# The experts' element work reordered, the router's tail moved behind the first expert's values, and the weighted down biases taken in one fp32r pass

## What is computed

```
x = x + attention(layernorm(x))
x = x + context_attention(layernorm(x), ctx, mask)
h = layernorm(x)                                  # the part that the change touches
logits = h @ router_weight.T + router_bias        # 512 x 16
top_val, top_idx = top_k(logits, 4)
scores = zeros.at[top_idx].set(softmax(top_val))  # 512 x 16, 4 of a row are not zero
gate, up = split(h @ gate_up[e] + gate_up_bias[e])
gate, up = min(gate, 7), clip(up, -7, 7)
out[e] = ((up + 1) * gate * sigmoid(1.702 * gate)) @ down[e] + down_bias[e]
x = x + sum over e of scores[:, e] * out[e]
```

## Time and profile before

| | us |
|---|---|
| median of 3 runs | 227.85 (227.73 to 227.97) |
| the profiled execution | 227.91 |
| its span, first to last instruction | 225.8 |
| around the span | 2.1 |
| PE busy | 215.7 (96%) |
| DVE busy | 176.1 (78%) |
| ACT busy | 125.6 (56%) |
| POOL busy | 84.3 (37%) |

### The profile page before, as it was taken

One profiled execution on the slowest core, in us unless ns is written; L12 is line 12 of the kernel. 1 busy time (PEld: TensorE's weight loads), 2 busy tenths in 40 slices (PEclk: granted clock), 3 DMA queues, 4 the chain that ended last, 5 costly groups with the idle time before them and its releaser, 6 DMA issues. The chain is left out here.

```text
span 225.8 us, 4387 instructions
## 1 busy us (share of the span) xinstructions
PE 215.7 (96%) x1394; PEld 175.9 (78%) x1394; DVE 176.1 (78%) x433; ACT 125.6 (56%) x248; POOL 84.3 (37%) x70
## 2 busy tenths in 40 slices
PE   7999999998997998899999999999999999999995
PEld 2688767776685987698797888888888887887894
DVE  3579887777768546888979879879879889889865
ACT  2239789778533219266466476385384484484540
POOL 6359989001011010443444435435426426425000
PEclk9999999999999999999999999999999999999999
DMA  6894420000000000040340340430421422310002
GB/s 181 328 378 140 141 86 0 0 4 0 3 0 0 3 0 1 0 142 20 122 129 12 139 126 17 139 101 38 139 77 62 139 64 75 139 46 0 0 0 93
DMA packets 7997, 17.41 MB, mean 77 GB/s; under 512 B 928, under 2 KB 3120, under 8 KB 7856
## 3 DMA queue, kind: packets, MB, share of 16 engines
q1 hardware_dynamic: 7552, 16.94, 22.9%
q10 hardware_dynamic: 432, 0.31, 0.4%
HBM read 16.72 MB, written 0.52 MB: 76 GB/s over the span
## 5 line engine op out<-in xcount | busy, mean ns | idle before, releaser
L307 POOL TENSOR_TENSOR WLg<-raw_g,WHg 128x1024 fp32r<-128x1024 f32 x16 | 38.3, 2394 | 49.8 <-ACT WHg L407 49.6
L837 DVE SCALAR_TENSOR_TENSOR pt<-pt 128x512 f32<-128x512 f32 x30 | 49.4, 1648 | 4.2 <-DVE pt L833 1.8
L536 ACT ACTIVATE HH<-pt 128x512 fp32r<-128x512 f32 x30 | 19.0, 632 | 53.1 <-DVE pt L837 53.0
L1155 PE MATMUL PS<-XH,WHg 128*128 128x512 f32 x120 | 47.0, 392 | 0.7 <-ACT pt L527 0.7
L1155 PE MATMUL PS<-XL,WHg 128*128 128x512 f32 x120 | 46.9, 391 | 0.0
L1155 PE MATMUL PS<-XH,WLg 128*128 128x512 f32 x120 | 46.7, 389 | 0.0
L1171 PE MATMUL PS<-WHd,HH 128*128 128x256 f32 x120 | 35.3, 294 | 1.5 <-DVE HL L842 1.1
L1171 PE MATMUL PS<-WLd,HH 128*128 128x256 f32 x120 | 33.9, 283 | 0.0
L1171 PE MATMUL PS<-WHd,HL 128*128 128x256 f32 x120 | 33.9, 283 | 0.0
L842 DVE TENSOR_TENSOR HL<-pt,HH 128x512 fp32r<-128x512 f32 x30 | 22.2, 739 | 11.0 <-ACT HH L536 11.0
L314 POOL TENSOR_TENSOR WLd<-raw_w,WHd 128x512 fp32r<-128x512 f32 x15 | 19.7, 1315 | 28.4 <-ACT WHd L413 28.3
(11 more groups left out here) (157 smaller groups left out, 349.2 us busy)
## 6 DMA issues: line engine op xcount, KB each, us to landing
raw_g<-we_d SPq DMA_DIRECT2D x16, 512.0 KB, 4.0
raw_w<-we_d SPq DMA_DIRECT2D x16, 256.0 KB, 2.7
ctxT<-ctxT_d SPq DMA_DIRECT2D x1, 1024.0 KB, 10.0
ctx_sb<-ctx_d SPq DMA_DIRECT2D x1, 1024.0 KB, 12.1
wqkv<-wqkv_d SPq DMA_DIRECT2D x3, 256.0 KB, 5.0
out_d<-x SPq DMA_DIRECT2D x4, 128.0 KB, 1.8
rows<-rows_d SPq DMA_DIRECT2D x1, 264.0 KB, 6.3
x<-x_d ACTq DMA_DIRECT2D x2, 128.0 KB, 3.2
```

The lines of the kernel that those rows point to most:

```text
L307: g.tensor_tensor(WLg[slot][:, :, :, :].rearrange("p k g f -> p (k g f)"), raw_g[slot][:, :], WHg[slot][:, :, :, :].rearrange("p k g f -> ...
L536: a.activation(HH[slot][:, m, :], hid[:, m, :], ACT.Copy).then_inc(hh_done, 1)
L837: v_.scalar_tensor_tensor(out=hid[:, m, :], in0=glu[:, m, :], scalar=GLU_MAX, in1=upc[:, m, :], op0=ALU.min, op1=ALU.mult).then_inc(hid_do ...
L1155: i = t.matmul(PS[:, 2 * m + part, :], w[slot][:, k, part, m * P:(m + 1) * P], xx[:, k, :], start=(n == 0), stop=(n == 3 * KD - 1))
```

## The change

1. **DVE's order in an expert** becomes product(0), product(1), low(0), low(1), and then all four of the weighted sum. **ACT's** becomes high(0), high(1), and only then the rounding of the gate_up weights of expert e + 2.
2. **The router's tail** (L810 to L817 of before) moves into expert 0's element work, behind low(1): it is `rest_of_router`.
3. **The exponential** is taken through a function that shares the GELU's table: with t = tanh(x / 8), ((1 + t) / (1 - t)) squared twice is exp(x). This adds six small DVE instructions. The table is loaded by name after the last exponential of the context attention.
4. **The scores and biases** get 80 rows in place of 16: scores high at rows 0 to 15, low at 32 to 47, high again at 64 to 79; biases high, high, low at the same rows. Both are fp32r, so that one product over 80 rows gives the three terms. DVE writes the score parts (three instructions), SP brings the biases three times, POOL clears the gaps and splits them (memsets at its start, three instructions 80x256 between its first and second `rstds`).
5. **PE** turns the scores behind down(0) (bank 6 in place of 5) and multiplies by the biases behind the first half of gate_up(2); DVE starts the accumulator in expert 1, behind low(1).

```diff
@@ SP @@
-            sp.dma_start(dbias[:, :], dbias_d).then_inc(dbias_in, 16)
+            sp.wait_ge(dbias_zero, 1)
+            for block in range(3):
+                sp.dma_start(dbias[block * 32:block * 32 + E, :], dbias_d).then_inc(dbias_in, 16)
@@ POOL @@
+            g.memset(dbias[:, :], 0.0).then_inc(dbias_zero, 1)
+            link(g.memset(low_rows[:, :], -1.0))
+            link(g.memset(low_rows[0:64, :], 0.0))
+            g.memset(score3[:, :, :], 0.0).then_inc(score3_zero, 1)
...
-            for n in range(1, 5):
-                rstds(n)
+            rstds(1)
+            pool.wait_ge(dbias_in, 48)
+            g.tensor_copy(dbias_high[:, :], dbias[:, :]).then_inc(dbias_split, 1)
+            pool.wait_ge(dbias_split, 1)
+            g.tensor_scalar(dbias_high[:, :], dbias_high[:, :].bitcast(F32), low_rows[:, 0:1], None, ALU.mult).then_inc(dbias_split, 1)
+            pool.wait_ge(dbias_split, 2)
+            g.tensor_tensor(dbias3[:, :], dbias[:, :], dbias_high[:, :].bitcast(F32), ALU.add).then_inc(dbias_split, 1)
+            rstds(2)
...
@@ ACT @@
             context_take(3)
+            a.preload_act_table_set("gelu_apprx_sigmoid_and_others")
...
-            a.activation(elog[:, :, :], dlog[:, :, :], ACT.Exp).then_inc(elog_done, 1)
+            a.activation(elog[:, :, :], dlog[:, :, :], ACT.Tanh, scale=0.125).then_inc(elog_done, 1)
...
                 high(0)
+                high(1)
                 if not isinstance(e, int) or e + 2 < E:
                     high_gate_up(e + 2, slot, pair + 1)
-                high(1)
@@ DVE @@
-            link(v_.tensor_tensor(within[:, :, :], rank[:, :, :], need[:, :].unsqueeze(2).to_broadcast([P, NC, E]), ALU.is_le))
...
+            def rest_of_router():
+
+                dve.wait_ge(elog_done, 1)
+                v_.tensor_scalar(root[:, :, :], elog[:, :, :], -1.0, 1.0, ALU.mult, ALU.add)
+                link(v_.tensor_tensor(within[:, :, :], rank[:, :, :], need[:, :].unsqueeze(2).to_broadcast([P, NC, E]), ALU.is_le))
+                v_.reciprocal(esel[:, :, :], root[:, :, :])
+                link(v_.tensor_tensor(sel_eq[:, :, :], eq[:, :, :], within[:, :, :], ALU.mult))
+                v_.scalar_tensor_tensor(out=root[:, :, :], in0=elog[:, :, :], scalar=1.0, in1=esel[:, :, :], op0=ALU.add, op1=ALU.mult)
+                link(v_.tensor_tensor(sel[:, :, :], sel_eq[:, :, :], gt[:, :, :], ALU.add))
+                link(v_.tensor_tensor(esel[:, :, :], root[:, :, :], root[:, :, :], ALU.mult))
+                link(v_.tensor_tensor(elog[:, :, :], esel[:, :, :], esel[:, :, :], ALU.mult))
...
+                link(v_.tensor_copy(high.bitcast(F32R), score[:, :, :]))
+                v_.tensor_tensor(low_, score[:, :, :], high, ALU.subtract)
+                v_.tensor_copy(again, high).then_inc(score_done, 1)
...
                 product(0)
+                product(1)
+                low(0)
+                low(1)
                 if isinstance(e, int) and e == 0:
+                    rest_of_router()
                     dve.wait_ge(scoreT_ps, 1)
-                    v_.tensor_copy(scoreT[:, :], PS[0:E, 5, :]).then_inc(scoreT_done, 1)
-                low(0)
-                product(1)
...
+                    v_.tensor_copy(scoreT[:, :], PS[0:ROWS3, 6, :]).then_inc(scoreT_done, 1)
+                if isinstance(e, int) and e == 1:
                     for c in range(NC):
                         dve.wait_ge(dbias_ps, c // 2 * 2 + 2)
...
-                else:
-                    weighted_sum(e - 1, 1 - slot, (0, 1))
-                    low(1)
-                    weighted_sum(e - 1, 1 - slot, (2, 3))
+                if not isinstance(e, int) or e >= 1:
+                    weighted_sum(e - 1, 1 - slot, range(NC))
@@ PE @@
-                    i = t.transpose(PS[0:E, 5, c * P:(c + 1) * P], score[:, c, :], ident[:, :])
+                    i = t.transpose(PS[0:ROWS3, 6, c * P:(c + 1) * P], score3[:, c, :], ident[:, :])
...
-                    if m == 0 and isinstance(e, int) and e == 1:
-                        turn_scores()
+                    if m == 0 and isinstance(e, int) and e == 2:
+                        weighted_biases()
...
+                down(e, slot)
                 if isinstance(e, int) and e == 0:
-                    weighted_biases()
-                down(e, slot)
+                    turn_scores()
```

More of the change, by code:

```diff
@@ L37 @@
 DW = D * KD
+ROWS3 = 2 * 32 + E
 def decoder_layer(nc, x_d, ctx_d, ctxT_d, wqkv_d, wo_d, params_d, rows_d, mask_d, dbias_d, we_d, out_d):
@@ L69, in decoder_layer @@
         mask8 = sb("mask8", [P, B * M], U8)
-        dbias = sb("dbias", [E, D])
+        dbias = sb("dbias", [ROWS3, D])
+        dbias_high = sb("dbias_high", [ROWS3, D], F32R)
+        dbias3 = sb("dbias3", [ROWS3, D], F32R)
+        low_rows = sb("low_rows", [ROWS3, 1])
         raw_g = [sb(f"raw_g{i}", [P, GU]) for i in range(2)]
@@ L133, in decoder_layer @@
         elog = sb("elog", [P, NC, E])
+        root = sb("root", [P, NC, E])
         esel = sb("esel", [P, NC, E])
@@ L137, in decoder_layer @@
         score = sb("score", [P, NC, E])
-        scoreT = sb("scoreT", [E, T])
+        score3 = sb("score3", [P, NC, ROWS3])
+        scoreT = sb("scoreT", [ROWS3, T], F32R)
         XH = sb("XH", [P, KD, T], F32R)
@@ L199, in decoder_layer @@
         out_done = sem("out_done")
+        dbias_zero, dbias_split, score3_zero, score_parts = (sem(n) for n in ("dbias_zero", "dbias_split", "score3_zero", "score_parts"))
         XS_BANK, XT_BANK, XV_BANK = (7, 2, 4, 5), (3, 4, 6, 3), (1, 2, 4, 5)
@@ L372, in _ @@
             split_keys(1)
-            for n in range(1, 5):
-                rstds(n)
+            rstds(1)
[6 more added lines that the diff above has]
+            rstds(2)
+            rstds(3)
+            rstds(4)
             def expert(e, slot, pair):
@@ L809, in _ @@
             link(i)
-            link(v_.tensor_tensor(within[:, :, :], rank[:, :, :], need[:, :].unsqueeze(2).to_broadcast([P, NC, E]), ALU.is_le))
-            link(v_.tensor_tensor(sel_eq[:, :, :], eq[:, :, :], within[:, :, :], ALU.mult))
-            link(v_.tensor_tensor(sel[:, :, :], sel_eq[:, :, :], gt[:, :, :], ALU.add))
-            dve.wait_ge(elog_done, 1)
-            link(v_.tensor_tensor(esel[:, :, :], elog[:, :, :], sel[:, :, :], ALU.mult))
-            link(v_.tensor_reduce(etot[:, :], esel[:, :, :], AX.X, ALU.add))
@@ L816, in _ @@
-            link(v_.reciprocal(erec[:, :], etot[:, :]))
-            v_.tensor_tensor(score[:, :, :], esel[:, :, :], erec[:, :].unsqueeze(2).to_broadcast([P, NC, E]), ALU.mult
-                             ).then_inc(score_done, 1)
+            def rest_of_router():
[8 more added lines that the diff above has]
+                link(v_.tensor_tensor(elog[:, :, :], esel[:, :, :], esel[:, :, :], ALU.mult))
+                link(v_.tensor_tensor(esel[:, :, :], elog[:, :, :], sel[:, :, :], ALU.mult))
+                link(v_.tensor_reduce(etot[:, :], esel[:, :, :], AX.X, ALU.add))
+                link(v_.reciprocal(erec[:, :], etot[:, :]))
+                link(v_.tensor_tensor(score[:, :, :], esel[:, :, :], erec[:, :].unsqueeze(2).to_broadcast([P, NC, E]), ALU.mult))
+                dve.wait_ge(score3_zero, 1)
+                high, low_, again = (score3[:, :, n * 32:n * 32 + E] for n in range(3))
+                link(v_.tensor_copy(high.bitcast(F32R), score[:, :, :]))
+                v_.tensor_tensor(low_, score[:, :, :], high, ALU.subtract)
+                v_.tensor_copy(again, high).then_inc(score_done, 1)
@@ L1141, in turn_scores, with weighted_biases @@
                 for c in range(NC):
-                    i = t.transpose(PS[0:E, 5, c * P:(c + 1) * P], score[:, c, :], ident[:, :])
+                    i = t.transpose(PS[0:ROWS3, 6, c * P:(c + 1) * P], score3[:, c, :], ident[:, :])
                 i.then_inc(scoreT_ps, 1)
+            def weighted_biases():
+                pe.wait_ge(scoreT_done, 1)
+                pe.wait_ge(dbias_split, 3)
+                for c in range(NC):
+                    t.matmul(PS[:, 6 + c // 2, (c % 2) * D:(c % 2 + 1) * D], scoreT[:, c * P:(c + 1) * P], dbias3[:, :], start=True, stop=True
+                             ).then_inc(dbias_ps, 1)
             def gate_up(e, slot):
@@ L1175, in down @@
                         i.then_inc(y_done, 1)
-            def weighted_biases():
-                pe.wait_ge(scoreT_done, 1)
-                pe.wait_ge(dbias_in, 16)
-                for c in range(NC):
-                    t.matmul(PS[:, 6 + c // 2, (c % 2) * D:(c % 2 + 1) * D], scoreT[:, c * P:(c + 1) * P], dbias[:, :], start=True, stop=True
-                             ).then_inc(dbias_ps, 1)
             def both(e, slot, pair):
```

1 line of the change is left out of this document (removed).

## The result

The kernel after takes 222.43 us (222.38 to 222.54, four runs) against 227.91 (227.73 to 228.24) for the kernel before in runs on the same chip: a ratio of 0.9759, with a 95% interval of 0.9742 to 0.9775. The forecast was 223.2, its range 220.7 to 226.0. The profiled execution took 222.38 us with a span of 220.7, against 227.91 and 225.8.

The account below looks back on a forecast made before the run. PE was taken to bound the kernel, paused each expert by a DVE, ACT and POOL ring; 1.59 - 0.48 - 0.25 + 3.82 = 4.68 us less gave 223.2 us, range 220.7 to 226.0 (80%).

Parts of the forecast that it names:

- accumulator's wait: In expert 1, down(1) waits for the accumulator's start at the end of DVE's list: 0.25 us lost, between 0 and 1.0.
- fourteen pairs: gate_up and down of experts from gate_up(2) on: 8.35 us a pair in place of 8.62, 3.82 us gained in all.
- Part 1: Expert loop: new order of element work on DVE and ACT removes PE's pause before down, 3.82 us gained.
- part 3: Expert 0: low(1) ends at 89.90, so down(0) runs from 91.7 to 94.6 without a wait; before, it started at 95.86.
- Part 2: Table load moves into ACT's idle stretch: expert 0's work comes 1.30 us earlier, PE's 0.69 wait goes, gate_up(1) at 86.2.
- Part 4: Behind down(0), PE waits 2.1 us for the scores (96.7); gate_up(2) starts at 97.25 against 98.84, 1.59 us gained.
- the hold: Router's tail: POOL's subtractions delay DVE rows reading two SBUF tiles; without this, the sum is 2.15 us lower.
- rival B: Router's tail: small DVE instructions aren't held by POOL, so PE has no pause before the scores; 221.0 us, 17%.
- C: Loop's seam: the 0.27 us pause is the price of wait values from registers and stays; 226.85 us, 15%.
- D: PE's pause at 94.6: the clock falls to its lower level; one pair at that level gives 231.6 us, 5%.
- E: Loop's first experts: part of the pause stays, where DVE is still late after the tail; 224 to 226 us, 8%.

Follow-up runs that it names:

- experiment 1: Kernel before with DVE's and ACT's new orders: 223.05 us; with DVE's alone: 224.17 us (profiled 223.34); with ACT's alone: 227.63 us.
- experiment 3: Kernel after with expert 1's down-weight subtraction behind the scores: 221.54 us; also with only 8 of 1024 columns subtracted for expert 2's gate_up: 220.76 us.
- experiment 8: Kernel before with 2080 unused bytes a partition ahead of the accumulator in SBUF: ratio 1.0009; its profiled execution took 228.43 us at mean clock 0.991.

## Why the prediction was right, step by step

| | forecast | measured |
|---|---|---|
| gate_up(1) starts | 86.2 | 86.03 |
| down(0) | 91.7 to 94.6 | 91.49 to 94.4 |
| scores there | 96.7 | 96.02 |
| turning | 0.5 | 0.39 |
| gate_up(2) earlier by | 1.59 | 2.37 |
| bias product | 0.48 lost | 0.47 |
| accumulator's wait | 0.25 lost | 0.12 |
| fourteen pairs, biases and wait apart | 3.82 gained | 3.89 |
| last addition to span's end | no change | 0.56 lost |
| around the span | no change | 0.43 gained |
| profiled time less by | 4.68 | 5.53 |

The two rows on the span's end weren't in the sum at all. That they nearly cancel is luck.

**Part 1** has the right size, and its mechanism half. That product(1) must not stand behind low(0) is shown (experiment 1); that ACT's late rounding, by taking POOL out of DVE's way, is part of the gain is refuted: with or without it the pair is 8.34. In the stretch ahead of gate_up(2) the order gives a further 0.66 (98.18 in place of 98.84 with the orders alone), which my sum had under part 3. So DVE's order alone brings the last block 4.6 us forward (219.56 to 214.97), and all the rest of the change, which is most of its lines, 1.1 (to 213.89).

**Part 2** held, where its experiment could be read. **Part 3** held to 0.2.

**Part 4** is the term that was mis-sized, by 0.78 us of the 0.85 that the sum missed. The held rows came as forecast, two of them, one for each POOL instruction. But POOL began 0.15 earlier than I had it and was done at 93.70, not 94.1; the rows that followed took 2.3, not 2.6 (they are ten, where I had counted eleven); and the turning 0.39, not 0.5. A slip without weight: 227.91 less 4.68 is 223.23, not 223.25. The price of the hold, with the tail in this place, is what the kernels of experiment 3 give back by their medians: 0.9 us without the second held row, 1.7 without either; by their ratios 1.0 and 2.0. gate_up(2) came 1.7 us earlier in the second, counted from gate_up(1). I had 2.15.

The Trainium skill's "SBUF — State Buffer", section "Who interferes with whom", gives no size from which its exclusion holds. The trace agrees with it down to 128x64 (2.05 us in place of 0.2), and rival B, that small rows escape, fell. With one SBUF input the reciprocal ran beside POOL undisturbed (0.55 with and without it), while the clip of 128x512, which has one too, was held (1.32 in place of 0.43). The same section has both: it exempts a single input, save in a mode with two ports, and counts tensor_scalar among the operations that can enter it.

**The rivals.** C (register waits make the seam's pause) fell: the loop still takes its wait values from registers and runs at 8.34, and in experiment 8 so do three of its pairs in the old order. D (the clock) fell for this kernel: 1.0 in all its four runs, with a pause of 1.55 us. But its argument against D, that the waits of before left no mark on the clock, held for one trace only: in experiment 8 the clock fell in a wait of 0.84 us, and the kernel without the early table load had one run at 0.854 and 238.94 us. E fell, since even the first pair behind gate_up(3) took 8.34.

## What to carry to other kernels

A pause of 0.2 us at each turn of a loop shows neither in PE's waits nor in its busy share. The page has only a hint of it, the idle time of PE's weight loads in front of down: 7.3 us before, 0.8 after. So subtract starts of blocks, and compare a turn that is unrolled with one in the loop. Where DVE and GpSimd meet on SBUF, look first at what stands behind the held instruction, because an order that does the multiplies of both halves before the first dependent step makes a hold of the same length harmless. Such a loop also hides what PE loses elsewhere, so a gain in front of it may only show once the loop is mended. Before moving work out of the way of a hold, follow what sets the other engine off: in two of the kernels above the hold came along, and in one it fell by itself into idle time.

## What the runs showed of the hardware

A DVE instruction of 128x64 with two SBUF inputs lasted 2.05 and 1.22 us beside GpSimd's subtractions and 0.16 to 0.23 otherwise. Between two back-to-back GpSimd instructions just one such DVE instruction got through, so each of the two cost a row. Both sides can lose: GpSimd's subtraction of 128x512 took 1.28 to 1.30 us mostly, but 1.75 where a held DVE subtraction ran between it and the long one (DVE's order alone), and 1.93 beside a DVE row that itself took 1.61 in place of 0.69. A reciprocal costs by width (0.55 us for 128x64, 0.18 for 128x4), where a multiply of 128x64 takes 0.22. Four matrix products of 16 rows by 128x256 in plain fp32 took 1.92 us where four of 80 rows in fp32r took 0.47. And the granted clock fell to its lower level (0.50) in one execution, within a wait of 0.84 us, where another with a wait of 0.81 at the same place kept the upper one.
